# The order of the shared expert's work among the routed quads, a new order of pieces in every step, and dt clipped by halves

## The reference

```python
# mixer: x -> x + mixer(layernorm(x))
xz = x @ in_proj_w.T;  xc, z = split(xz)
u = causal_conv(xc, 4 taps, 256 -> 256 channels) + conv_b
dt = clip(sigmoid(u @ dt_w.T + dt_b), 1e-4, 1.0)
Bm = u @ B_w.T;  Cm = u @ C_w.T                        # 16 states
dA = exp(clip(dt[:, :, None] * A, -5, 5))
state = dA * state + dt * Bm * u + 1e-6                # along time, 256 channels x 16 states
y = sum_n(state * Cm) + D * u
out = (y * silu(z)) @ out_w.T
# experts: x -> x + ffn(layernorm(x))
shared = (silu(xt @ sg_w.T) * (xt @ su_w.T)) @ sd_w.T
probs = sigmoid(xt @ router_w.T + bias);  top 2 of 8 experts, shares normed to 1
out = shared + sum over the 2 experts of share * expert(xt)   # hidden size 256
```

## Time and profile before

| | us |
|---|---|
| median of 3 runs | 1402.33 |
| lowest, highest | 1399.95, 1402.63 |
| the profiled execution | 1403.58 |
| its span, from first to last instruction | 1401.9 |
| TensorE busy | 1217.3 |
| VectorE busy | 1177.6 |
| ScalarE busy | 901.7 |
| GpSimd busy | 847.7 |
| granted TensorE clock, share of full | 0.973 |

### The profile page before, as it was taken

How to read it: one execution, slowest core, us unless ns; L and a number is a source line. 1 busy time by engine, 2 the same in 40 slices (tenths; PEclk the granted TensorE clock), 3 DMA queues, 4 the chain that set the end, 5 groups by cost and what they waited for, 6 DMA issues and landing times.

```text
span 1401.9 us, 27101 instructions
## 1 busy us (share of the span) xinstructions
PE 1217.3 (87%) x8709; PEld 1022.8 (73%) x8709; DVE 1177.6 (84%) x2236; ACT 901.7 (64%) x1452; POOL 847.7 (60%) x1354
## 2 busy tenths in 40 slices
PE   6779897899989898998989898998989999787883
PEld 3556676687777777787877777777777877777873
DVE  0799999998898979998898979998898989988323
ACT  4766665577775866876776867777577676763321
POOL 3444545844377764768567774767647773755454
PEclk9999999999999999999999999999999999999997
DMA  6000000032324143133423242143412333355783
GB/s 178 1 1 9 1 9 9 20 117 73 109 82 127 35 143 108 41 124 99 121 63 118 62 143 87 56 130 89 130 61 68 112 95 98 95 174 178 244 274 89
DMA packets 111646, 132.29 MB, mean 94 GB/s; under 512 B 10128, under 2 KB 82704, under 8 KB 111504
## 3 DMA queue, kind: packets, MB, share of 16 engines
q1 hardware_dynamic: 98416, 111.31, 25.6%
q0 software_dynamic: 8192, 16.79, 4.2%
q10 hardware_dynamic: 4896, 2.43, 0.6%
HBM read 102.37 MB, written 28.11 MB: 93 GB/s over the span
## 4 chain that ended last, share of the span: by engine, by line
PE 42%; DVE 26%; ACT 13%; issue 11%; DMA 3%; POOL 3%; SPq 1%; DVEq 0%; POOLq 0%; ACTq 0%
DVE h L1279 11%; DVE yT L1297 10%; PE p_hT L1053 7%; PE p_db L1036 7%; PE p_misc L1060 6%; PE p_dn L1216 4%; PE p_gu L1204 4%; ACT dA L872 3%; PE p_gu L1195 3%; ACT L969 2%; ACT hm L969 2%; PE p_misc L1097 2%; POOL ysel L791 2%; ACT dBT L929 2%; PE p_misc L1113 1%
## 5 line engine op out<-in xcount | busy, mean ns | idle before, releaser
L1279 DVE TENSOR_TENSOR_SCAN h<-dA,p_db 128x512 f32<-128x512 f32 x512 | 603.7, 1204 | 66.1 <-PE p_db L1036 64.7
L735 POOL TENSOR_SCALAR dBT<-wT,bcT 128x256 f32<-128x256 f32 x704 | 340.1, 483 | 347.8 <-ACT wT L903 138.0
L1297 DVE SCALAR_TENSOR_TENSOR yT<-p_hT,bcT,yT 128x256 f32<-128x256 f32 x960 | 402.9, 471 | 40.4 <-PE p_hT L1053 40.4
L872 ACT ACTIVATE dA<-dt_sb,A_sb 128x510 f32<-128x510 f32 x512 | 333.0, 711 | 27.7 <-DVE h L1279 26.4
L1036 PE MATMUL p_db<-ident,dBT 128*128 128x128 f32 x2048 | 300.8, 278 | 57.0 <-DVE h L1279 53.3
L1036 PEld LDWEIGHTS p_db<-ident,dBT 128*128 128x128 f32 x2048 | 238.5, 143 | 112.9 <-issue 102.9
L1053 PE MATMUL p_hT<-ident,h 128*128 128x128 f32 x2048 | 290.2, 281 | 25.3 <-DVE yT L1297 14.0
L1053 PEld LDWEIGHTS p_hT<-ident,h 128*128 128x128 f32 x2048 | 237.9, 145 | 64.6 <-issue 31.5
L929 ACT ACTIVATE dBT<-wT,eps,bcT 128x256 f32<-128x256 f32 x320 | 163.9, 592 | 0.0
L777 POOL DMA_INDIRECT xs_dram<-xn,slot x128 | 127.4, 995 | 54.7 <-issue 35.9
L791 POOL DMA_INDIRECT ysel<-ys_dram,slot x128 | 123.8, 968 | 56.5 <-issue 32.4
(11 more groups left out here) (189 smaller groups left out, 1485.6 us busy)
## 6 DMA issues: line engine op xcount, KB each, us to landing
wring<-w_moe_dram SPq DMA_DIRECT2D x169, 384.0 KB, 4.3
xt<-xs_dram SPq DMA_DIRECT2D x41, 256.0 KB, 5.2
ys_dram<-yo SPq DMA_DIRECT2D x34, 256.0 KB, 2.3
dA<-w_moe_dram SPq DMA_DIRECT2D x16, 384.0 KB, 5.8
x_sb<-x_dram SPq DMA_DIRECT2D x16, 256.0 KB, 4.1
out_dram<-x SPq DMA_DIRECT2D x15, 256.0 KB, 2.5
xs_dram<-ysel SPq DMA_DIRECT2D x4, 512.0 KB, 6.2
xs_dram<-xn,slot POOLq DMA_INDIRECT x128, 2.3
```

The costliest lines, as they stand in the source:

```text
L735: op = pool.tensor_scalar(dBT[:, j % DBT_RING, c], wT[:, g % 2, c], bcT[:, g % 2, c, n:n + 1], STATE_EPS, ALU.mult, ALU.add)
L872: act.activation(dst[:, :, 1:], src[:, :, 1:], ACT.Exp, scale=A_sb[:, half, n:n + 1]).then_inc(exp_done, 1)
L1279: dve.tensor_tensor_scan(h[:, j % 2, half], dA[:, j % DA_RING, half], p_db[half][:], 0.0, ALU.mult, ALU.add).then_inc(scan_done, 1)
L1297: op = dve.scalar_tensor_tensor(yT[:, g % 2, cc], p_hT[pair][:, c], bcT[:, g % 2, cc, NS + n:NS + n + 1], yT[:, g % 2, cc], ALU.mult, ALU.add)
```

## The change

It has six parts.

- `quad_order()` takes a due shared quad ahead of routed ones, as long as the unit is below `SHARED_FIRST` = 224. The shared quads of groups 3, 5, 7, 9 and 11 come 12 units earlier, and three routed quads of batches 0 to 4 each come 4 units later. Every group from 4 to 13 then has three routed quads and one shared one. With the last routed quad, the gathers, additions and stores of these batches come 4 units later. From unit 217 on the row of quads is the one of before.
- The tables of all steps have new orders. On PE, U of step 3 stands behind i0, v0 and i1, ahead of X; u1 goes from behind h to step 4, ahead of h; G stands ahead of i0 in step 5; the two G of step 10 stand at the end of step 9; i0 of the next group's first unit stands in step 14 ahead of h. On ACT, d6 stands behind u0, E ahead of V, m1 ahead of d3, and sig behind x.
- `KINDS`: unit 9 of each group is made by ACT, so 6 of 16 instead of 5.
- dt is clipped by halves: clip0 needs only dt0, and each half of w needs only its half of dt.
- dt0 now waits for u0 alone, and its rest f0 for u1. This matters in group 0 only, since later the one bank keeps them in order anyway. The wait for the mixer's weights goes from u0 to dt0.
- Before group 0, z0 and z1 stand behind the transposes of the first unit.

```diff
-KINDS = "pppsspspppppppss"
+KINDS = "pppsspsppsppppss"
...
+SHARED_FIRST = NS * (GROUPS - 2)
...
-        at = next(i for i, (ready, _) in enumerate(waiting) if ready <= cursor)
+        at = min((i for i, (ready, _) in enumerate(waiting) if ready <= cursor),
+                 key=lambda i: (waiting[i][1][0] != "shared" or cursor >= SHARED_FIRST, i))
...
-            def clip_dt(g):
-                pool.wait_ge(misc_emptied, max(misc_at["dt0", g], misc_at["dt1", g]))
-                pool.tensor_scalar(dt_sb[:, g % 2], dt_sb[:, g % 2], 1.0, DT_MIN, ALU.min, ALU.max
+            def clip_dt(g, half):
+                pool.wait_ge(misc_emptied, misc_at[f"dt{half}", g])
+                pool.tensor_scalar(dt_sb[:, g % 2, half], dt_sb[:, g % 2, half], 1.0, DT_MIN, ALU.min, ALU.max
                                    ).then_inc(dt_ready, 1)
...
             def weigh_u(g, half):
 
+                pool.wait_ge(dt_ready, HALVES * g + half + 1)
                 if half == 0:
-                    pool.wait_ge(dt_ready, g + 1)
...
                 if name in ("u0", "u1"):
                     convolve(g, half, 1).then_inc(misc_in_psum, 1)
                 else:
+                    pe.wait_ge(misc_emptied, misc_at["u1", g])
...
                 if name == "u0" and g == 0:
-                    pe.wait_ge(mixer_weights, 16 * len(mixer_loads))
...
                 if name in ("dt0", "dt1"):
                     half = int(name[2])
-                    pe.wait_ge(misc_emptied, misc_at["u1", g])
+                    if g == half == 0:
+                        pe.wait_ge(mixer_weights, 16 * len(mixer_loads))
+                    pe.wait_ge(misc_emptied, misc_at["u0", g])
```

More of the change, by code:

```diff
@@ L68 @@
 PE_SLOTS = (
[5 rows of a table removed]
[L74 removed]
[5 rows of a table removed]
[5 rows of a table added]
+DVE_SLOTS = (
[5 rows of a table added]
 ACT_SLOTS = (
[3 rows of a table removed]
[3 rows of a table added]
 POOL_SLOTS = (
[L85 to L87 removed]
[3 rows of a table added]
 SP_SLOTS = (
[L89 to L90 removed]
+    "", "T T W Y O W W", "", "O Y xl W O Y Y O T", "", "T T T O Y W W W", "", "Y T W O Y Y O O", "",
+    "T T O W T W", "", "Y Y O Y W O O W T T W", "", "W", "T Y T O O Y Y O O", "W W Y Y T T")
 PE_FIRST = (
[1 row of a table removed]
[1 row of a table added]
     "h i0 i1 N G U X", "h i0 i1 N G U X", "h i0 i1 N G U X", "h i0 i1 N G U X", "h i0 i1 N G U X",
     "h i0 i1 N G U X", "h i0 i1 N G U X", "h i0 i1 N G U X", "h i0 i1 N G U X", "h i0 i1 N G U X",
[1 row of a table removed]
[1 row of a table added]
 DVE_FIRST = (
@@ L104 @@
 POOL_FIRST = (
-  "clip w0 w1", "c d S", "c d S", "c d S", "c d S", "c d S", "c d S", "c d S", "c d S", "c d S", "c d S",
-  "c d S", "c d S", "c d S", "c d S", "c d S", "c d S")
+    "clip0 w0 clip1 w1", "c d S", "c d S", "c d S", "c d S", "c d S", "c d S", "c d S", "c d S", "c d S",
+    "c d S", "c d S", "c d S", "c d S", "c d S", "c d S", "c d S")
 SP_FIRST = (
@@ L826, in _ @@
                                    ln2_mv, ln2_step, xn2_ready)
-                    if name == "clip" and ahead is not None:
-                        clip_dt(ahead)
+                    if name in ("clip0", "clip1") and ahead is not None:
+                        clip_dt(ahead, int(name[4]))
                     if name in ("w0", "w1") and ahead is not None:
@@ L864, in decays @@
                 if n == 0:
-                    act.wait_ge(dt_ready, g + 1)
+                    act.wait_ge(dt_ready, HALVES * (g + 1))
                 if j == 0:
```

5 lines of the change are left out of this document (removed), and 33 rows, old and new, of tables (ACT_SLOTS, DVE_SLOTS, PE_FIRST, PE_SLOTS).

## The result

| | before | after |
|---|---|---|
| median of the runs compared, us | 1401.14 | 1431.52 |
| runs | 4 (1399.76 to 1402.63) | 4 (1429.44 to 1433.68) |
| span of the profiled execution | 1401.9 | 1427.7 |
| group 6 / group 7, first scan to first scan | 84.4 / 75.8 | 89.5 / 77.0 |
| last scan of group 15 | 1288.7 | 1312.8 |

The ratio is 1.0209, with a 95% interval of 1.0193 to 1.0224. I had forecast 1394 us, with 1407 as the upper end of the range.

What follows compares the result with a forecast made beforehand. No single engine bounds it: PE, with ACT behind it, owns steps 3 to 8 of a group, DVE the rest. 5.0 - 0.5 + 1.0 + 1.5 + 1.5 = 8.5 us gained, giving 1394 us, range 1384 to 1407.

Steps and rivals of the forecast that it cites:

- What costs nothing: Later gathers, dBT of unit 9 on ACT, d12 and SP's moved stores and loads were to cost no time.
- Even groups: Groups 4 to 12: PE's pause at X goes, u1 loses its cover; net gain 1.0 each, 5.0 us in five.
- Odd groups: Groups 5 to 13: X of routed quad 5 added, u1 loses its cover; net loss 0.1 each, 0.5 us in all.
- Group 14: Routed quads alone: 1.52 from PE's pause less 0.45 for u1's lost cover, gain 1.0 us.
- Group 15: Exponentials and silu ahead of the router shorten U's waits for ACT: gain 1.5 us, bounds 0 and 4.0.
- The start: Earlier convolution and dt0, clip by halves: first scan 2.4 earlier, 0.8 given back; gain 1.5 us, bounds 0 and 2.4.
- The tail: After the groups: its tables and quads are the same, so it shifts as a whole.
- Table loads: ACT's loads go from 135 to 148 at 1.28 us each; the skill's drain would make the sum 4.5 us worse.
- the rivals: Nothing is left: 1401, chance 0.21; PE pays and gets nothing: 1409, 0.15; ACT's relief works everywhere: 1386, 0.14.
- the slower ones: Chiefly PE pays and gets nothing: u1's lost cover, odd groups' X, ACT late for xnT; 1405 to 1414, chance 0.15.

Runs made afterwards that it cites:

- e2: The changed kernel with the old choice of quads (shared quads in order of readiness), pieces, start and clip still changed: 1421.44 us, ratio 1.0133.
- the repaired kernel: The changed kernel with POOL's instructions cut into quarters and i0 behind h14 again: 1400.62 us (ratio 0.9968), on another chip 1397.80 (0.9956).

## Why the prediction was wrong

**What costs nothing** is the part that failed. I moved the gathers, and with them POOL's weighting and additions, into steps 9 to 11 of the even groups, and asked only whether POOL would be in time for PE. The other end of the question, whom POOL hinders by working there, wasn't asked. DVE is busy for 22 us longer by it: 13 with the gathers' new place, the other 9 with the new order, which puts w0 beside rest (e2). Of the time, cutting POOL's instructions gave back 9 us beside the changed kernel and 17 once i0 was back, and the forecast had nothing for it. The cost could be seen in the trace of before, in one place. There w0 and w1 run beside the router of group 2, DVE's row first:

```profile
218.71 1.17 DVE L1353 TENSOR_TENSOR key<-key,rank 128x64 f32<-128x64 f32 x1
```

```profile
217.30 2.50 POOL L758 TENSOR_TENSOR w_sb<-dt_sb,u_sb 128x512 f32<-128x512 f32 x2
```

The mean of that group is 389 ns over 14; six others take 224 to 226 ns, and seven, which stand beside POOL's dBT, 411 to 421. A row that stands five times above its kin was the sign to look for.

**i0 ahead of h14** had no term at all in my sum, and is the second step that failed. The order showed it; I counted it as a move inside a stretch that DVE owns. It was worth 16 to 17 us in the changed kernel and 12 in the kernel before.

**Even groups** (forecast: 1.0 gained each). With both causes out, group 6 takes 84.1, so 0.3 is gained. X runs without a wait, and u1 waits for DVE's x, as forecast (0.34 here, 0.45 forecast). Timeline of PE after the change, steps 3 and 4:

```profile
498.01 0.60 PE L1165 MATMUL p_misc<-ident,xt 128*128 128x128 f32 x4
...
504.28 1.99 PE L1063 MATMUL p_misc<-xnT,wtap 128*128 128x512 f32 x4 [0.34 <-DVE x L1310]
```

From group 6's first scan to unit 9 the repaired kernel needs 48.2 us against 48.0, with 1.2 of stats1 now behind that first scan: PE's part gains 1.0 where I had 1.6. The rest loses 0.7; I had 0.6. What I mis-sized is PE's gain, by a third; which piece of it is missing I haven't isolated.

**Odd groups** (0.1 lost each): 76.4 in all but one against 75.9 to 76.5, so 0.5 lost at most; that one is group 5, 77.8 against 75.9, 2.0 lost, which I haven't followed up. **Group 14** (1.0 gained): repaired 85.1 against 83.2, 1.9 lost; this one is wrong in sign, and no run was made for it. **Group 15** (1.5 gained, up to 4.0): 6.4, above my upper bound. Sigmoid's place gives 3.0 of it, the other 3.4 come with the order of its pieces and aren't told apart further. **The start** (1.5 gained): the end of group 0 comes 1.7 earlier in the changed kernel, 0.8 and 3.1 in the repaired ones; right in size, with a spread as large as itself. **The tail** (shifts as a whole): 1.7 us longer in the profiled execution; open.

**Table loads**: at their 1.28 us and off the path, as forecast from the earlier trace rows; the rows show no drain.

In all, with the lock and i0 repaired, the kernel has 6.2 us less than before on one chip and 3.1 on another, where my sum had 8.5. But this is a sum of errors of both signs, group 15's 4.9 too little among them, so that it comes near my sum is in part luck. None of the rivals named either cause: the slower ones had PE waiting for ACT, or PE's own added work.
